# Second layer of a two-layer attention and expert program: the f16 copy of the exponentials moves from ScalarE to GpSimd, and GpSimd's features get a wait for each pair

## What is computed

```
e      = relu(rho(q[:, :, None, :] + k[:, None, :, :]))     # signed square root: sqrt of the positive part
scores = einsum('bija,a->bij', e, Wphi)
ex     = exp(scores - max(scores))
denom  = sum(ex)
part1  = einsum('bij,bjc->bic', ex, Vy)
Ew     = einsum('bij,bija->bia', ex, e)
part2  = einsum('bia,ca->bic', Ew, We_w) + We_b * denom
out    = (part1 + part2) / (denom + 1e-9)
```

## Time and profile before

| | |
|---|---|
| median of 3 runs | 1418.5 us |
| lowest, highest | 1409.52, 1418.61 us |
| the profiled execution | 1419.44 us, its span 1417.7 us |
| mean granted TensorE clock | 0.971 |
| busy, of the span | PE 86%, DVE 87%, ACT 80%, POOL 62% |
| second layer's loop | from about 430 us to the end; one block takes 30.6 us |

### The profile page before, as it was taken

One profiled execution on the slowest core, in us unless ns is written; L12 is line 12 of the kernel. 1 busy time (PEld: TensorE's weight loads), 2 busy tenths in 40 slices (PEclk: granted clock), 3 DMA queues, 4 the chain that ended last, 5 costly groups with the idle time before them and its releaser, 6 DMA issues.

```text
span 1417.7 us, 24950 instructions
## 1 busy us (share of the span) xinstructions
PE 1215.6 (86%) x6185; PEld 581.0 (41%) x6185; DVE 1233.1 (87%) x3409; ACT 1135.6 (80%) x1292; POOL 879.3 (62%) x1294
## 2 busy tenths in 40 slices
PE   3899999996758888888888888888888888888887
PEld 2577666664522333333333333333333333333334
DVE  5767888887648899999999999999999999999997
ACT  1776888884259899989999899999898999988950
POOL 0754633331005787778877877878777887787830
PEclk9999999998668999999999999999999999999998
DMA  5001100000000000000000010000000000000001
GB/s 188 9 11 27 25 1 0 0 1 1 19 0 15 20 19 19 22 26 26 19 18 19 18 30 26 19 18 19 18 28 20 26 19 18 18 19 30 26 19 34
DMA packets 38786, 31.66 MB, mean 22 GB/s; under 512 B 6150, under 2 KB 35609, under 8 KB 38738
## 3 DMA queue, kind: packets, MB, share of 16 engines
q1 hardware_dynamic: 37714, 29.76, 7.2%
q0 software_dynamic: 1024, 1.35, 0.6%
HBM read 29.10 MB, written 2.75 MB: 22 GB/s over the span
## 4 chain that ended last, share of the span: by engine, by line
DVE 32%; PE 28%; issue 9%; DVEq 3%; ACT 1%; POOL 0%; ACTq 0%
DVE arena L1051 18%; PE ps L1331 9%; PE ps L1344 8%; DVE arena L1037 6%; PE ps L1388 4%; PE ps L1408 2%; PE ps L1380 2%; DVE x L1094 2%; PE ps L1362 2%; DVE z L1077 2%; DVE spread L1103 2%; DVE nmax L1043 1%; DVEq L1050 1%; DVEq L1094 1%; ACT arena L1188 1%
## 5 line engine op out<-in xcount | busy, mean ns | idle before, releaser
L1051 DVE SCALAR_TENSOR_TENSOR arena<-arena,ps 128x512 f32<-128x512 f32 x1024 | 662.8, 679 | 66.0 <-PE ps L1344 65.7
L1188 ACT ACTIVATE arena<-arena,eps 128x4096 f32<-128x4096 f32 x128 | 474.1, 3707 | 38.6 <-POOL arena L1311 38.1
L1305 POOL TENSOR_SCALAR arena<-kT,negq 128x512 f32<-128x512 f32 x480 | 331.5, 702 | 196.9 <-DVE arena L1051 181.5
L1344 PE MATMUL ps<-spread,sel 128*128 128x512 f16 x1024 | 348.3, 386 | 118.4 <-DVE arena L1051 112.0
L1311 POOL TENSOR_SCALAR arena<-arena,q 128x512 f32<-128x512 f32 x480 | 351.0, 741 | 22.4
L1344 PEld LDWEIGHTS ps<-spread,sel 128*128 128x128 f16 x1024 | 92.2, 97 | 512.1 <-DVE arena L1051 437.4
L1331 PE MATMUL ps<-arena,phi_cols 128*32 128x512 f32 x2048 | 276.4, 614 | 20.2 <-ACT arena L1188 20.2
L1176 ACT ACTIVATE arena<-kT,q 128x512 f32 (+1 forms) x330 | 217.2, 712 | 3.3 <-issue 0.3
L462 POOL TENSOR_SCALAR kT<-kT,region 128x512 f32<-128x512 f32 x128 | 88.9, 694 | 155.5 <-DVE region L587 154.3
L1037 DVE TENSOR_SCALAR arena<-kT,q 128x512 f32 (+1 forms) x214 | 141.3, 683 | 0.3 <-PEq L789 0.3
L512 ACT ACTIVATE kT<-ps,region 128x512 f32<-128x512 f32 x128 | 88.1, 688 | 59.1 <-DVE region L582 56.4
(11 more groups left out here) (196 smaller groups left out, 1723.7 us busy)
## 6 DMA issues: line engine op xcount, KB each, us to landing
wge<-in_e_wg SPq DMA_DIRECT2D x32, 256.0 KB, 2.7
w1e<-in_e_w SPq DMA_DIRECT2D x32, 128.0 KB, 2.1
w2e<-in_e_w SPq DMA_DIRECT2D x32, 128.0 KB, 2.1
w3e<-in_e_w SPq DMA_DIRECT2D x32, 128.0 KB, 2.1
region<-in_w SPq DMA_DIRECT2D x1, 2048.0 KB
out<-x SPq DMA_DIRECT2D x4, 256.0 KB, 2.8
region<-in_wqk SPq DMA_DIRECT2D x1, 512.0 KB, 4.8
region<-in_wv SPq DMA_DIRECT2D x1, 512.0 KB, 5.4
```

What stands on the lines that cost most here:

```text
L1051: dve.scalar_tensor_tensor(feat[:, j, k, :], feat[:, j, k, :], 1.0, psB[:, k % BANKS, :], ALU.mult, ALU.mult, accum_out=sums[:, j, gg, c:c ...
L1188: act.activation(grp, grp, ACT.Sqrt, bias=eps[:]).then_inc(e_ready, 2)
L1305: pool.tensor_scalar(feat[:, j, QUADS * gg + c, :], kT[:, b * N:(b + 1) * N], HUGE, negq[:, b % 2, at - b * N // 2:at - b * N // 2 + 1], A ...
L1344: pe.matmul(psB[:, k % BANKS, :], sel[:, gg, c, :], spread[:, j, :], start=True, stop=True).then_inc(bc_done, 1)
```

## The change

ScalarE's second exp (L1200) is removed. GpSimd gets `halve`, a copy of `ex` to `exh` with the cast to f16, ahead of its `lift`. GpSimd's features are now pairs c = 0 and 1 of each group, and each cut waits for the reduction of its own pair, where both waited for the group's four. VectorE's feature is c = 2 in place of 0, ScalarE's keep the last places. `place` stands behind the features of group 7, not ahead of them. The scores of the next block wait for `ex` alone to leave their PSUM bank.

```diff
--- before.py
+++ after.py
@@ -1032,7 +1032,7 @@
             def _(dve):
                 def feature(m, j, gg, c, ahead=False):
 
-                    if ahead or c < ON_DVE[gg]:
+                    if ahead or ON_POOL[gg] <= c < ON_POOL[gg] + ON_DVE[gg]:
                         b, pair0 = slot_parts(m)
                         dve.tensor_scalar(feat[:, j, QUADS * gg + c, :], kT[:, bass.ds(b * N, N)],
                                           q2[:, bass.ds(pair0 + GROUPS * c + gg, 1)], 0.0,
@@ -1195,9 +1195,6 @@
                         act.wait_ge(exT_done, m - 1)
                         act.wait_ge(spread_ready, m - 1)
                     act.activation(ex[:, j, :], psS, ACT.Exp, bias=shift[:, j:j + 1]).then_inc(ex_ready, 1)
-                    if before:
-                        act.wait_ge(spread_ready, m)
-                    act.activation(exh[:], psS, ACT.Exp, bias=shift[:, j:j + 1]).then_inc(exh_ready, 1)
 
                 def keep_exT(m, j, warm=True):
                     act.wait_ge(exT_done, m + 1)
@@ -1274,9 +1271,16 @@
                         if m or h:
                             pool.wait_ge(placed, 2 * m + h)
                         pool.wait_ge(lifted, (m + 1) * GT)
-                        made = min(m * sum(ON_POOL) + sum(ON_POOL[:-1]), (MB - 2) * sum(ON_POOL))
+                        made = min(m + 1, MB - 2) * sum(ON_POOL)
                         pool.wait_ge(pool_feat, made)
                         pool.tensor_copy(v[h * A:(h + 1) * A, :, :, h], sums[h * A:(h + 1) * A, j]).then_inc(placed, 1)
+
+                def halve(m):
+
+                    pool.wait_ge(ex_ready, m + 1)
+                    if m:
+                        pool.wait_ge(spread_ready, m)
+                    pool.tensor_copy(exh[:], ex[:, m % 2, :]).then_inc(exh_ready, 1)
 
                 def lift(m):
 
@@ -1290,17 +1294,17 @@
 
                     b, j = m // BB, m % 2
                     before = (m - 2) * sum(ON_POOL) + sum(ON_POOL[:gg])
-                    mine = range(ON_DVE[gg], ON_DVE[gg] + ON_POOL[gg])
+                    mine = range(ON_POOL[gg])
+                    if gg == 0 and m > 2:
+                        pool.wait_ge(placed, 2 * (m - 2))
                     if before == 0 or (m % BB == 0 and gg == 0):
                         if b > 1:
                             pool.wait_ge(pool_cut, before - BB * sum(ON_POOL))
                         pool.tensor_scalar(negq[:, b % 2, :], q2[:, b * N // 2:(b + 1) * N // 2], -1.0, None,
                                            ALU.mult).then_inc(negq_ready, 1)
                         pool.wait_ge(negq_ready, b + 1)
-                    if gg == GROUPS - 1:
-                        pool.wait_ge(placed, 2 * (m - 1))
-                    pool.wait_ge(reduced, (m - 2) * PAIRS + QUADS * (gg + 1))
                     for c in mine:
+                        pool.wait_ge(reduced, (m - 2) * PAIRS + QUADS * gg + c + 1)
                         at = m * PAIRS + GROUPS * c + gg
                         pool.tensor_scalar(feat[:, j, QUADS * gg + c, :], kT[:, b * N:(b + 1) * N], HUGE, negq[:, b % 2, at - b * N // 2:at - b * N // 2 + 1],
                                            ALU.min, ALU.max).then_inc(pool_cut, 1)
@@ -1310,23 +1314,23 @@
                         pool.wait_ge(pool_cut, before + n + 1)
                         pool.tensor_scalar(f, f, 1.0, q2[:, at:at + 1], ALU.mult, ALU.add).then_inc(pool_feat, 1)
 
+                halve(0)
                 for m in range(MB):
                     for gg in range(GROUPS):
                         if gg == LIFT_AT:
+                            if m + 1 < MB:
+                                halve(m + 1)
                             lift(m)
-                        if gg == GROUPS - 1 and m + 2 < MB:
-                            place(m)
                         if m + 2 < MB:
                             features(m + 2, gg)
-                    if m + 2 >= MB:
-                        place(m)
+                    place(m)
 
             @block.tensor
             def _(pe):
                 def scores(m, j, gg, first=False):
                     pe.wait_ge(e_ready, m * GROUPS + gg + 1)
                     if gg == 0 and not first:
-                        pe.wait_ge(exh_ready, m)
+                        pe.wait_ge(ex_ready, m)
                     for c in range(QUADS):
                         ins = pe.matmul(psS[32 * c:32 * (c + 1), :], phi_cols[:, gg, :],
                                         feat[:, j, QUADS * gg + c, :], start=(gg == 0), stop=(gg == GROUPS - 1))
```

## The result

The changed kernel takes 1405.6 us (median of 17), the one before 1414.6 beside it; the ratio is 0.994 with an interval of 0.9925 to 0.9956. It is faster by 0.6%, 9 us. The forecast was 1420, +1.5 us on a base of 1418.5, the median of the 3 runs known then; the 17 runs of now put that base at 1414.6, so 4 of the 14 us between 1420 and 1405.6 lie in the base. The time lies in the range and the change is under the 1% that was called no change, but it is clear of the noise and goes the other way. The profiled execution took 1409.26 us, 10.2 less than the one of before.

What follows compares the result with a forecast made beforehand. VectorE's stretch from (3,0) to (7,3) and a part fixed by TensorE make the period in turns. The steps mostly cancel to +0.05 us a block, 30 × 0.05 = +1.5 us, giving 1420 us; range 1401 to 1437.

Steps and rivals of the forecast that it cites:

- Step 1: VectorE's feature of group 0 moves from behind (1,0) to behind (1,2) and the product z: in TensorE's part, 0.
- Steps 2 and 3: VectorE's feature moves from (3,0) to (3,2), +0.45 us a block; and from (4,0) to (4,2), −0.45.
- Step 4: VectorE's feature moves from (6,0) to (6,2), meeting GpSimd's second lift: −0.46 us if VectorE is ahead, otherwise 0.
- the branch (lift ahead): At (6,2), GpSimd's second lift starts before VectorE's feature, ends near 949.75, and (6,3) stands where it stood: 0.
- Step 5: Feature moves from (7,0) to (7,2), and the split: with the lift ahead, split loses 0.05 at most, (7,3) at +0.05.
- The cast, priced at 0 as covered: GpSimd's cast between group 5's features and the lifts: taken as 0.65 us, lifts still in time, so covered.
- The finer waits, priced at 0: GpSimd's features c = 0 and 1 each wait for their own reduction; not waited for on the path: 0.
- The walk: Five steps through one block, following VectorE's moved features with other pitches kept: three of four branches end at +0.05 us.
- The signs: Expected profile: ScalarE's feature waits gone, VectorE idle about 0.5 us ahead of (3,2), feature 0.47 at (4,2), 0.47 or 0.9 at (6,2).
- the slower case: Split and feature before (7,3) meet GpSimd instructions just begun: half of both 1435 us, both in full 1450; chance 0.17.
- The rival with ScalarE as the pace: ScalarE sets the period, so dropping its second exp gives 21 us, to 1398, or 1361 with its waits; chance 0.08.
- The slower rival: At the block's end, VectorE's split and (7,2) feature wait behind GpSimd: 1435 us at half, 1450 in full; chance 0.17.

Runs made afterwards that it cites:

- the two last: Changed kernel, cast ahead of group 5, VectorE's pairs [[2],[],[1],[],[],[2],[2],[2]]: 1364.3 us; then group 6's feature moved to group 7: 1355.2 us.

## Why the prediction was wrong

*What bounds the kernel*: right. VectorE's stretch and TensorE's take turns, ScalarE is off the path. The six kernels built on this reading (the earlier cast, one feature to group 7, both, group 2's one pair earlier, and the two last) came out 0.6 to 4.2 us above what it put down for them.

*Step 1*, "in TensorE's part, 0", is the step that failed. TensorE's rows were read as one run without a gap, and they are; but one of them, the product at 931.99, was 1.13 long and started late, since it waited for z. The view of waits had it (11.5 us, 28 times), but among the weight loads, and the prediction read the waits of the matmuls alone. The stretch gave −0.18 us a block, 5.5 us in 30 blocks; moving the feature behind z alone gave 4.7 us. In the changed kernel 0.14 of the 0.18 would have come without that move, from the feature no longer meeting a cut.

*Steps 2 and 3*: right to 0.04 us. *Step 4*: the branch (lift ahead) was right, its end wrong by 0.15: the cast starts before its row's predecessor has ended and adds 0.58 to the chain, not 0.65, so the lift ended earlier under VectorE's feature: −0.17 in place of 0, 5 us in 30 blocks. That is as much as step 1, and either one alone turns the forecast's +0.05 into a gain; step 1 had the mechanism wrong, step 4 only the size. *Step 5*: +0.08, forecast +0.05.

*The cast, priced at 0 as covered*, costs 11 us by the phase that it gives the lifts. The walk contains that cost, in the lift under which the feature at (6,2) starts, and so came out near; but "covered" was the wrong word for it, and the text did not say that the same cast is free in front of group 5. *The finer waits, priced at 0*: without them, and with the cast, the kernel takes 24 us more; what they cover was named nowhere.

*Outside the walk*: 2.1 us in the loop's first block, with the clock. Some 1 us lies ahead of the first split (431.1 and 430.45) and in block 0, and was not traced to a cause.

*The signs.* VectorE waits 0.41 ahead of (3,2) (forecast 0.5), the feature at (4,2) lasts 0.51 (0.47), and that at (6,2) lasts 0.78, neither 0.47 nor 0.9. The split above 0.8 us, which was to show the slower case, came too (0.83) in a kernel that is faster: the sign was too weak to tell. The period fell while the wait ahead of (1,0) stayed at 1.48, since what got shorter in TensorE's part lies behind (1,0).

The rival with ScalarE as the pace is refuted twice. The slower rival is real but not here: its place, the split with two SBUF inputs, loses 0.08 in the changed kernel and 0.45 in the one with the group's wait. The Trainium skill, SBUF — State Buffer, "Who interferes with whom", has the second to issue blocked in full. The traces agree that VectorE's instruction then ends only behind GpSimd's, but it is not held up from its own start: a split that started 0.04 behind a cut of 0.69 lost 0.45, not the 0.65 that were left of the cut.

## What to carry to other kernels

Where two engines take turns, find the stretches first; an instruction costs its whole pitch in its engine's own stretch and nothing in the other's, unless something there waits for it (the feature ahead of z cost 0.18), so the place of a filler is worth more than its duration. A row that is longer than its like inside a busy engine's run can hide a wait: compare durations, not only gaps, and read the waits of the weight loads too. Where two engines share a port, an added instruction must be followed to the phases behind it, and its first candidate is the engine's idle gap.

## What was not expected of the hardware

An idle stretch of TensorE of about 2 us could be followed by some 3 us at a granted clock of 0.5, at 1.2 GHz, and need not be. Before, 2.19 us of idle ahead of the loop's first block was followed by it; with the cast alone, nearly all blocks behind the first idle 2.08 us and eight had the fall; with the group's wait, nearly all idle 1.89 and eight had it. Such a block took 1.2 to 2.0 us longer than its neighbours. After 1.55 us of idle in every block of the kernel before, and 1.09 in every block of the changed one, nothing fell. Why some idle stretches of the same length are followed by the fall and others are not stays open. GpSimd's copy with a cast from f32 to f16 takes 615 ns for 128x512, about what its lift takes (612 before, 627 in the changed kernel).
